# A decoder's second-layer self attention as a skewed pipeline, with its state sums in summing order and its squares on ScalarE

## What is computed

```python
q, k, v = (qkv[:, :, 0], qkv[:, :, 1], qkv[:, :, 2])
Z = jnp.einsum('bhsd,de->bhse', k, W0)
y1, vjp1 = jax.vjp(ln_f, Z)
dz1 = vjp1(y1 - v)[0]
KK = mask * jnp.einsum('bhtd,bhsd->bhts', k, k)
Z2 = Z - jnp.einsum('bhts,bhsd->bhtd', KK, dz1)
y2, vjp2 = jax.vjp(ln_f, Z2)
dz2 = vjp2(y2 - v)[0]
A = mask * jnp.einsum('bhtd,bhsd->bhts', q, k)
ctx = jnp.einsum('bhsd,de->bhse', q, W0) - jnp.einsum('bhts,bhsd->bhtd', A, dz1 + dz2)
```

## Time and profile before

| | |
|---|---|
| median of 3 runs | 6312.41 us (6308.8 to 6314.84) |
| the profiled execution | 6316.28 us, its span 6314.5 us |
| VectorE busy | 3620.7 us, 57% of the span |
| TensorE busy with products | 3596.9 us, 57% |
| ScalarE busy | 1577.1 us, 25% |
| GpSimd busy | 749.3 us, 12% |

### The profile page before, as it was taken

How to read it: one execution, slowest core, us unless ns; L and a number is a source line. 1 busy time by engine, 2 the same in 40 slices (tenths; PEclk the granted TensorE clock), 3 DMA queues, 4 the chain that set the end, 5 groups by cost and what they waited for, 6 DMA issues and landing times. The chain is left out here.

```text
span 6314.5 us, 71361 instructions
## 1 busy us (share of the span) xinstructions
PE 3596.9 (57%) x21570; PEld 2472.5 (39%) x21634; DVE 3620.7 (57%) x10096; ACT 1577.1 (25%) x3714; POOL 749.3 (12%) x1030
## 2 busy tenths in 40 slices
PE   4679999534346601601533344489978887833333
PEld 4456666312114400501422233356656665523222
DVE  2453333688896530554577755444446665567776
ACT  1452232100004300200111111233324443423332
POOL 0240000000003257075000000000000000000000
PEclk9789999766668755555655556589989999966666
DMA  3000000000000000300200000000000000000000
GB/s 80 4 10 5 10 10 5 8 0 0 0 0 12 16 2 1 84 1 3 59 0 0 0 6 0 7 3 10 7 14 0 0 0 3 0 10 0 0 0 13
DMA packets 84128, 60.48 MB, mean 10 GB/s; under 512 B 21067, under 2 KB 78744, under 8 KB 83332
## 3 DMA queue, kind: packets, MB, share of 16 engines
q1 hardware_dynamic: 67164, 56.87, 3.2%
q0 software_dynamic: 12288, 0.68, 0.2%
q10 hardware_dynamic: 4608, 2.10, 0.1%
HBM read 64.98 MB, written 19.14 MB: 13 GB/s over the span
## 5 line engine op out<-in xcount | busy, mean ns | idle before, releaser
L398 DVE TENSOR_TENSOR l_ffn_h<-l_ffn_sg,l_ffn_p_u 128x512 f32<-128x512 f32 (+1 forms) x448 | 308.0, 688 | 408.2 <-PE l_ffn_p_u L371 406.6
L387 ACT ACTIVATE l_ffn_sg<-l_ffn_p_g 128x512 f32<-128x512 f32 (+1 forms) x448 | 267.5, 597 | 819.0 <-PE l_ffn_p_g L368 805.0
L371 PE MATMUL l_ffn_p_u<-l_ffn_f_xTall,l_ffn_wu 128*128 (+1 forms) x896 | 461.2, 596 | 8.4 <-DVE l_ffn_h L398 8.4
L368 PE MATMUL l_ffn_p_g<-l_ffn_f_xTall,l_ffn_wg 128*128 (+1 forms) x896 | 461.8, 597 | 1.9 <-DVE l_ffn_f_logits L259 1.0
L377 PEld LDWEIGHTS l_ffn_p_o<-l_ffn_wd,l_ffn_h 128*128 128x128 f32 (+1 forms) x3584 | 410.3, 192 | 31.0 <-issue 31.0
L377 PE MATMUL l_ffn_p_o<-l_ffn_wd,l_ffn_h 128*128 128x128 f32 (+1 forms) x3584 | 410.6, 275 | 0.0
L95 POOL TENSOR_TENSOR rstd<-vareps,minus_half 128x32 f32<-128x32 f32 x12 | 65.2, 5435 | 2860.9 <-DVE vareps L86 2134.2
L994 PE MATMUL l_attn_p_s<-l_attn_outer,l_attn_upper 128*128 128x512 f32 x256 | 191.7, 917 | 298.5 <-DVE l_attn_outer L905 232.0
L407 DVE SCALAR_TENSOR_TENSOR x<-l_ffn_p_o,l_ffn_cw,x 128x128 f32 x512 | 171.2, 351 | 284.2 <-PE l_ffn_p_o L377 282.4
L2675 PE MATMUL l_ffn_p_sim<-ident,l_ffn_w 128*128 128x128 f32 x128 | 35.6, 433 | 481.8 <-DVE l_ffn_w L2623 481.8
L371 PEld LDWEIGHTS l_ffn_p_u<-l_ffn_f_xTall,l_ffn_wu 128*128 128x128 f32 (+1 forms) x896 | 166.2, 186 | 230.5 <-issue 221.3
(11 more groups left out here) (690 smaller groups left out, 8992.1 us busy)
## 6 DMA issues: line engine op xcount, KB each, us to landing
l_attn_toep<-kernel_rows SPq DMA_DIRECT2D x1, 8192.0 KB, 31.5
ssm_toep<-ssm_rows SPq DMA_DIRECT2D x1, 8192.0 KB, 31.4
l_slots_w<-in_L_ffn_w SPq DMA_DIRECT2D x32, 176.0 KB, 2.3
slots_in<-l_route_xd,l_route_at POOLq DMA_INDIRECT x192
l_combine_got<-slots_out,l_combine_at POOLq DMA_INDIRECT x192
l_slots_w<-in_L_ffn_w SPq DMA_DIRECT2D x32, 88.0 KB
x<-in_x SPq DMA_DIRECT2D x1, 2048.0 KB
l_ffn_wg<-in_L_ffn_w_gate SPq DMA_DIRECT2D x8, 256.0 KB, 2.7
```

The source lines that it names most:

```text
L368: pe.matmul(X.p_g[0:X.FP, k % 2], X.wg[:, w, f * X.FP:(f + 1) * X.FP], x, start=True, stop=True).then_inc(s.gate_psum, 1)
L371: pe.matmul(X.p_u[0:X.FP, k % 2], X.wu[:, w, f * X.FP:(f + 1) * X.FP], x, start=True, stop=True).then_inc(s.up_psum, 1)
L387: act.activation(X.sg[:, k % 2], X.p_g[0:X.FP, k % 2], ACT.Silu).then_inc(s.silu_ready, 1)
L398: dve.tensor_tensor(X.h[:, k // X.FC, k % X.FC], X.sg[:, k % 2], X.p_u[0:X.FP, k % 2], ALU.mult).then_inc(s.h_ready, 1)
```

## The change

The layout of the state products becomes (head, j, i), with i innermost, so the sum over i reads neighbours. Gain and minus sign of the layer norm are folded into the projection's weights, as is the removal of z's mean (a second set of blocks, `bdc`); group norm's gain goes into `Wout`, its offset through `Wout` into the output's bias. The projection's bias comes from a product of a row of ones with `bproj`, one row deep, added in the buffer. ScalarE copies the projection out and squares, both between its other copies. GpSimd adds the output's bias to x. The loop becomes `skewed` with depth 3 over the 16 pairs: 19 items, in each of which pair t is projected and gets its first gradient, t - 1 its first states and second gradient, t - 2 its second states and group norm, and t - 3 its output. Four items stand ahead of a loop of three times four, and three behind it. The buffer `p_s` still has two halves, used by turns for the second states of t - 2, the first of t - 1 and the projection of t. The core of the diff:

```diff
+                pool.wait_ge(s.composed, 2)
+                for item in skewed(pool, 3, PAIRS):
+                    for b, u in item(2):
+                        after(pool, s.out_taken, b)
+                        pool.tensor_tensor(side(xb[:]), pair(R.x, b), both(bout), ALU.add).then_inc(s.xb_ready, 1)
...
+                chain(dve.tensor_reduce(means[:], heads(bd[:]), AX.X, ALU.add))
+                chain(dve.scalar_tensor_tensor(out=heads(bdc[:]), in0=means[:].unsqueeze(2).broadcast_to((P, H, HD)), scalar=-1.0 / HD,
+                                               in1=heads(bd[:]), op0=ALU.mult, op1=ALU.add))
+                chain(dve.tensor_tensor(bproj[:, W:3 * P], bproj[:, W:3 * P], lnb[:], ALU.subtract))
+                for t in (wproj, bproj):
+                    chain(dve.scalar_tensor_tensor(out=t[:, W:3 * P], in0=t[:, W:3 * P], scalar=-1.0, in1=g[:, 0:P], op0=ALU.mult, op1=ALU.mult))
+                dve.tensor_tensor(g2[:], g[:], g[:], ALU.mult).then_inc(s.blocks_ready, 1)
...
-                def centred(u, var_ready):
-
-                    chain(dve.tensor_reduce(st[:, u, 0], heads(z[u]), AX.X, ALU.add))
-                    chain(dve.tensor_scalar(st[:, u, 0], st[:, u, 0], 1.0 / HD, None, ALU.mult))
-                    chain(dve.tensor_tensor(heads(n_[:, u]), heads(z[u]), wide(st[:, u, 0]), ALU.subtract))
-                    chain(dve.tensor_tensor(t1[:, u], n_[:, u], n_[:, u], ALU.mult))
-                    chain(dve.tensor_reduce(st[:, u, 1], heads(t1[:, u]), AX.X, ALU.add))
-                    dve.tensor_scalar(st[:, u, 1], st[:, u, 1], 1.0 / HD, EPS, ALU.mult, ALU.add).then_inc(var_ready, 1)
...
                     chain(dve.reciprocal(m[:, 1], m[:, 1]))
-                    chain(dve.tensor_tensor(heads(n), heads(n), wide(m[:, 1]), ALU.mult))
-                    chain(dve.tensor_tensor(d, n, g[:], ALU.mult))
-                    chain(dve.tensor_tensor(d, d, minus_w[u], ALU.subtract))
-                    chain(dve.tensor_tensor(d, d, g[:], ALU.mult))
+                    chain(dve.tensor_tensor(heads(n), heads(zc), wide(m[:, 1]), ALU.mult))
+                    chain(dve.tensor_tensor(d, n, g2[:], ALU.mult))
+                    chain(dve.tensor_tensor(d, d, v, ALU.add))
                     chain(dve.tensor_tensor(t, d, n, ALU.mult))
                     dve.tensor_reduce(m[:, 2], heads(d), AX.X, ALU.add)
                     chain(dve.tensor_reduce(m[:, 3], heads(t), AX.X, ALU.add))
-                    chain(dve.tensor_scalar(m[:, 2:4], m[:, 2:4], 1.0 / HD, None, ALU.mult))
-                    dve.tensor_tensor(heads(d), heads(d), wide(m[:, 2]), ALU.subtract)
-                    chain(dve.tensor_tensor(heads(n), heads(n), wide(m[:, 3]), ALU.mult))
-                    chain(dve.tensor_tensor(d, d, n, ALU.subtract))
-
-                def outer_products(u, dz, ready):
+                    dve.scalar_tensor_tensor(out=heads(d), in0=wide(m[:, 2]), scalar=-1.0 / HD, in1=heads(d), op0=ALU.mult, op1=ALU.add)
+                    chain(dve.scalar_tensor_tensor(out=heads(n), in0=wide(m[:, 3]), scalar=-1.0 / HD, in1=heads(n), op0=ALU.mult, op1=ALU.mult))
+                    chain(dve.tensor_tensor(d, d, n, ALU.add))
...
-                                          over_rows(x[u][:, r * P:(r + 1) * P]), ALU.mult).then_inc(s.slot_read, 1)
-                    dve.wait_ge(s.slot_read, i * USES + (use + 4))
-                    chain(dve.tensor_reduce(step[:, u].rearrange("p (h j) -> p h j", j=HD),
-                                            part[:].rearrange("p r (h i j) -> p (r h) j i", i=HD, j=HD), AX.X, ALU.add))
-
-                with dve.Fori(0, NB // 2 // U) as i:
+                                          over_columns(x[:, r * P:(r + 1) * P]), ALU.mult).then_inc(read, 1)
+                    dve.wait_ge(read, b * 2 + 2)
+                    chain(dve.tensor_reduce(step, part[:].rearrange("p r (m i) -> p (r m) i", i=HD), AX.X, ALU.add))
...
+                        dve.wait_ge(s.sq2_ready, b + 1)
+                        dve.tensor_reduce(st2[:, 0], heads(t2[:]), AX.X, ALU.add).then_inc(s.var2_ready, 1)
+                    for b, u in item(2):
+                        dve.wait_ge(s.sq3_ready, b + 1)
+                        dve.tensor_reduce(gs[:, 1], heads(t3[:]), AX.X, ALU.add).then_inc(s.squares_ready, 1)
+                    for b, u in item(0):
+                        dve.wait_ge(s.sq1_ready, b + 1)
+                        dve.tensor_reduce(st1[:, 0], heads(t1[:]), AX.X, ALU.add).then_inc(s.var1_ready, 1)
...
+                            dve.tensor_tensor(square(outer2[:, r]), over_columns(k_[u][:, r * P:(r + 1) * P]),
+                                              over_rows(dz2[:, r * P:(r + 1) * P]), ALU.mult).then_inc(s.outer2_ready, 1)
...
+                        act.wait_ge(s.proj_psum, b * 2 + 1)
+                        act.activation(proj[:, u, 0:3, 0], p_s[:, 0, 0, 0:3 * P].rearrange("p (c n) -> p c n", n=P), ACT.Copy)
+                        act.activation(proj[:, u, 3:5, 0], p_s[:, 0, 1, 0:W].rearrange("p (c n) -> p c n", n=P), ACT.Copy).then_inc(s.proj_read, 1)
+                    for b, u in item(1):
+                        act.wait_ge(s.z2_ready, b + 1)
+                        act.activation(t2[:], z2[:], ACT.Square).then_inc(s.sq2_ready, 1)
+                    for b, u in item(2):
+                        act.wait_ge(s.centred_ready, b + 1)
+                        act.activation(t3[:], qw[u], ACT.Square).then_inc(s.sq3_ready, 1)
...
+                        act.activation(proj[:, u, 0:3, 1], p_s[:, 1, 0, 0:3 * P].rearrange("p (c n) -> p c n", n=P), ACT.Copy)
+                        act.activation(proj[:, u, 3:5, 1], p_s[:, 1, 1, 0:W].rearrange("p (c n) -> p c n", n=P), ACT.Copy).then_inc(s.proj_read, 1)
+                        act.wait_ge(s.proj_read, b * 2 + 2)
+                        act.activation(t1[:], z[u], ACT.Square).then_inc(s.sq1_ready, 1)
+                    for b, u in item(1):
+                        act.wait_ge(s.var2_ready, b + 1)
+                        act.activation(st2[:, 1], st2[:, 0], ACT.Sqrt, scale=1.0 / HD, bias=eps[:]).then_inc(s.std2_ready, 1)
...
+                def projected(b, r):
+                    after(pe, s.part1_read, b * 2 + (r - 1))
+                    for c, cols in ((0, slice(0, 3 * P)), (1, slice(3 * P, 5 * P))):
+                        wide_ = cols.stop - cols.start
+                        pe.matmul(p_s[:, r, c, 0:wide_], xT[:, r * P:(r + 1) * P], wproj[:, cols], start=True, stop=False)
+                        mm = pe.matmul(p_s[:, r, c, 0:wide_], R.ones[0:1, :], bproj[0:1, cols], start=False, stop=True)
+                    mm.then_inc(s.proj_psum, 1)
...
+                for item in skewed(pe, 3, PAIRS):
+                    for b, u in item(2):
                         for r in range(2):
+                            for c, _ in item(1):
+                                pe.wait_ge(s.proj_read, c * 2 + (r + 1))
+                            states(b, r, s.outer2_ready, s.states2_psum, outer2)
+                    for b, u in item(1):
+                        for r in range(2):
+                            after(pe, s.part2_read, b * 2 + (r - 1))
+                            states(b, r, s.outer1_ready, s.states1_psum, outer1)
```

253 lines of the change are left out of this document (125 added, 128 removed).

## The result

| | median, us | runs, us | profiled execution, us | its span, us |
|---|---|---|---|---|
| before | 6313.6 | 4, 6308.8 to 6316.5 | 6316.3 | 6314.5 |
| changed | 6138.6 | 4, 6134.7 to 6147.1 | 6147.1 | 6145.3 |
| forecast | 6128 | 6092 to 6182 | 6132.0 | |

The changed kernel is faster: 0.9725 of the time before, 95% interval 0.9708 to 0.9742. On two later occasions its median was 6129.1 and 6137.7 us, so the forecast of 6128 lies at the lower edge of what is measured.

The account below looks back on a forecast made before the run. VectorE's program was taken to bound the loop. Work 477, full-item waits 23.4 and ends 29.2 make 529.6 us against 716.2; with 2.3 before it, 184.3 less: 6132.0 profiled, 6128 us median, range 6092 to 6182.

Parts of the forecast that it names:

- VectorE's work in the loop: VectorE's own work over the 16 pairs of the changed loop: 29.8 us a pair, 477 us in all.
- added before the loop: Seven small VectorE operations and a fifth product ahead of the loop: about 2.3 us more.
- The removed work: VectorE work dropped per pair in sums, bias adds, centring, gradient and group norm: 11.04 us.
- The waits that take their place: VectorE's new waits per item: 0.7 for first-layer states, none for output, 0.9 for z's square; about 1.6 us.
- I take 0.2 an item: GpSimd's output-bias add slows VectorE instructions beside it: 0.2 us an item.
- The hard reading: VectorE stands for GpSimd's whole add in the loop: 13 us in all instead of 3, time 6138 us.
- The ends: VectorE's waits in the first three and last three items, where cover is missing: 29.2 us.
- The projection at the low clock: Rival: TensorE's projection runs at the low clock, 7.3 us an item instead of 1.8; 6199 us; chance 0.22.
- The kept price: Rival: VectorE's sums over state products stay at 3.8 us despite the new order; 6177 us; chance 0.05.
- The engines in series: Rival: the shared score buffer puts TensorE and VectorE in series, 52.4 us an item; 6466 us; chance 0.02.
- What it said would show: Phase signs: VectorE busy near 456 us, sum 2.29, items 31 to 32 apart, waits 1 to 2, full-clock projection, one table load.

Follow-up runs that it names:

- The order alone: Kernel before, with only the tiles of products laid out in summing order, so the sum reads neighbours: 6271.9 us, 0.9931 of before.
- the arithmetic in the old schedule: Kernel before with summing order, folded weights, shorter gradient, squares and roots on ScalarE; bias still on VectorE, no skew: 6185.4 us, 0.9791 of before.
- the run with unread products: Changed kernel with eight unread 256-column products per item in TensorE's idle stretch ahead of the first layer's states: 6125.1 us, 4.0 less.
- the moved sum: Changed kernel with z's sum of squares (L946) moved behind the second gradient, and ScalarE's second root moved: 6107.8 us, 21.3 less than the changed kernel.

## Why the prediction was right, point by point

The phase was forecast 184.3 us shorter and is 174.6 shorter, 9.7 us less than forecast. By its own terms:

| term, us | forecast | measured |
|---|---|---|
| VectorE's work in the loop (length less waits) | 477 | 479.2 |
| waits, full items | 20.8 | 24.9 |
| GpSimd's add, full items | 2.6 | 0 |
| waits at both ends | 29.2 | 34.2 |
| added before the loop | 2.3 | 2.0 |
| hand-over to the next phase (idle before L1138) | 0 | 1.3 more |

- **The removed work** (11.04 us a pair) was right part by part: the sum's 2286 ns, the fused scalings at the price of plain ones, large products unchanged. The order alone and the arithmetic in the old schedule bear it out with 49.3 and 138.5 us.
- **The waits that take their place** sum nearly to the forecast, and that is in part luck: 13 x 1.6 = 20.8 us of waits and 13 x 0.2 for GpSimd were put, 24.9 and nothing came. The 13 full items wait 17.2 us for z's square, 5.9 for the first layer's states and 1.7 for the output. That is 1.3, 0.45 and 0.13 an item where I had 0.9, 0.7 and nothing, and the wait for states isn't in every item: four have 1.2 to 1.4 us of it, one 0.6 and eight none. In the item of the timeline the square is there 16.5 us after the start (1420.82), to the tenth as forecast, by two errors that cancel: the projection begins at 8.9 and not at 10.3, since states of 5.4 us take the place of my mean of 6.0 and the steps behind them are short, and each half takes 2.9 us where "2.1 at the full one" stood. What moved is VectorE: it is there at 15.1 and not at 15.6, having waited less for states and not at all for GpSimd, so it waits that much more for the square.
- **"I take 0.2 an item" for GpSimd** is the step whose mechanism failed, though it cost only 2.6 us of the sum. I averaged over a slowdown that is all or nothing: 0.4 us for an elementwise instruction with two SBUF inputs that stands beside the add, and nothing beside statistics, where the change puts it. The row that it was taken from, L1151, is also of another kind, a TENSOR_SCALAR with one tile as input. The hard reading that I set beside it, the add's whole length for 13 us, is wrong for this place too, but near what the add costs beside the gradient (7 to 9 us), where VectorE does stand until the add ends.
- **The ends** are the largest error of the sum, 5.0 us. The first item waits 13.6 us for the square and 1.2 for the root, behind ScalarE's table load, where I had 11.4; the second 7.5 for 6; the third 4.0 for 2.7. At the far end 7.8 us stand against 9.1.
- **The rivals.** The projection at the low clock did not come: the clock is 1.00 over the window, and without its one-row products the phase only gained. Its mechanism is real, though, as two items of the run with unread products show. Its sum has a slip that changes nothing: states that end at 9.4 and are wanted at 8.0 make a wait of 1.4, not 1.6, and the output then waits that much longer. The kept price is refuted by the order alone. The engines in series did not come; the longest wait of a full item is 1.5 us.
- What it said would show, shows: VectorE busy 460.6 us (456), the sum at 2.29, most full items 31.4 us apart and some 32.7 (those with a wait for states), one load of the table, 1.3 us of waiting at L946. The wait at L934 did not come every time but in 10 of 16 items.
- **The rest of the program**, which I left at its price, was 5.4 us longer in the profiled execution. That is scatter, as three profiles of one kernel show.

## What to carry to other kernels

Price a sum by the step of its addresses, and choose the layout of what is summed for the reader when the writer doesn't care: it was a quarter of the gain for a handful of lines. After a change of schedule, look for the instruction that waits for the longest chain and ask what independent work could stand ahead of it; here one sum moved 7 us later gave another 17 to 25 us. Put GpSimd's work beside VectorE's sums, statistics and reads of PSUM, never beside elementwise work on two SBUF tiles, and count what stands beside it, not how long it is.

## What the runs showed of the hardware that was not expected

- GpSimd's adds double VectorE's elementwise instructions with two SBUF inputs (0.42 to 0.83 us), slow a TENSOR_SCALAR with one (a pair from 0.60 to 1.00) and leave sums and reads of PSUM alone; a loop with GpSimd busy 407 of 679 us lost 143 us.
- A faster item can make its own products slower: with the moved sum the idle stretches ahead of the states fell from 7.7 to 6.5 and from 5.0 to 4.4 us, and the bursts still went from 5.4 to 6.0 us. With unread products in those stretches they take 3.6 to 3.7 us at 2.4 GHz, so the low clock was costing 1.7 us a burst in the changed kernel and 2.3 after the sum was moved.
- A product with one row costs TensorE what one with 128 rows does (0.84 us for 384 columns), yet without them the loop's mean clock is 0.67 instead of 0.73 and the states come later.
- Code that was not touched varies by 22 us between executions, and 14 of them are one phase, whose length follows its granted clock (256.8 us at 0.81, 242.9 at 0.88). So an effect of 10 us in one phase is better read from that phase than from the total.
